# Gated cross-attention and RWKV feed-forward: the first layer norm folded into the query weights and the score bias, queries in 512-column products

## The reference

```python
xn = layernorm(x)                                   # (x - mean) / sqrt(var + 1e-5), no weights
Q, K, V = xn @ W_q.T, ctx @ W_k.T, ctx @ W_v.T      # 16 heads of 32
s = Q @ K.T / sqrt(32) - slope[head] * (qpos - kpos)        # masked keys: -inf
e = exp(s - max(s)); attn = e / (1 + sum(e))
x = x + tanh(g_xattn) * ((attn @ V) @ W_o.T)
y = layernorm(x); y_prev = y shifted by one token
xr, xk = mu_r * y + (1 - mu_r) * y_prev, mu_k * y + (1 - mu_k) * y_prev
x = x + tanh(g_ffn) * sigmoid(xr @ W_r.T) * (relu(xk @ W_k2.T) ** 2 @ W_v2.T)
```

## Time and profile before

| | |
|---|---|
| median of 3 runs | 1484.07 us (1483.07 to 1484.63) |
| profiled execution | 1483.82 us, of which its span 1482.0 us |
| busy: TensorE, weight loads | 1381.9 us (93%), 1087.4 us (73%) |
| busy: VectorE, ScalarE, GpSimd | 1009.0 us (68%), 887.6 us (60%), 717.5 us (48%) |
| mean granted clock of TensorE | 0.991 of full speed |
| x tiles loaded | 64 of 256 KB, 3.0 us from issue to landing |

### The profile page before, as it was taken

One profiled execution on the slowest core, in us unless ns is written; L12 is line 12 of the kernel. 1 busy time (PEld: TensorE's weight loads), 2 busy tenths in 40 slices (PEclk: granted clock), 3 DMA queues, 4 the chain that ended last, 5 costly groups with the idle time before them and its releaser, 6 DMA issues.

```text
span 1482.0 us, 33624 instructions
## 1 busy us (share of the span) xinstructions
PE 1381.9 (93%) x10864; PEld 1087.4 (73%) x10864; DVE 1009.0 (68%) x3658; ACT 887.6 (60%) x2931; POOL 717.5 (48%) x766
## 2 busy tenths in 40 slices
PE   7999899899999989999998989999999999999988
PEld 6876768677776867767686767767686777778667
DVE  5435858586685858677585868769585866858565
ACT  5247375665747466574747567474756657474652
POOL 0103555645545554655545464545556455455542
PEclk9999999999999999999999999999999999999999
DMA  8721001020100102010010202010020202001000
GB/s 267 222 76 43 15 21 60 0 64 14 57 21 28 50 0 78 0 57 21 28 50 14 64 0 57 21 46 32 16 62 0 64 14 57 21 28 50 4 27 29
DMA packets 53010, 65.96 MB, mean 45 GB/s; under 512 B 23024, under 2 KB 29168, under 8 KB 52976
## 3 DMA queue, kind: packets, MB, share of 16 engines
q1 hardware_dynamic: 52976, 65.52, 15.2%
HBM read 40.87 MB, written 24.64 MB: 44 GB/s over the span
## 4 chain that ended last, share of the span: by engine, by line
PE 43%; DVE 17%; issue 15%; POOL 9%; ACT 9%; DMA 5%; SPq 0%; DVEq 0%; POOLq 0%; ACTq 0%
PE rotating L401 27%; PE probs_bank L561 8%; ACT probs L775 5%; PE attn_bank L575 4%; POOL square L1368 4%; DVE diff L1109 3%; POOL xnt_or_act L1370 3%; DVE relu L1109 3%; DMA xs<-in_x_dram 2%; DVE square L1104 2%; PE score_bank L401 2%; DVE norm L1026 2%; POOL probs L1331 1%; DVE mix_k L1104 1%; POOL mixed_key L1358 1%
## 5 line engine op out<-in xcount | busy, mean ns | idle before, releaser
L775 ACT ACTIVATE probs<-probs,neg_max 128x120 f32<-128x120 f32 x1024 | 391.0, 386 | 19.6 <-DVE neg_max L1048 19.6
L1331 POOL TENSOR_TENSOR probs<-probs,recip 128x960 f32<-128x960 f32 x128 | 229.4, 1792 | 259.9 <-DVE recip L1062 259.9
L401 PE MATMUL rotating<-mixed_key,w_key 128*128 128x512 f32 x720 | 197.7, 414 | 36.5 <-ACT gated L827 36.5
L401 PE MATMUL rotating<-w_proj,attn_t 128*128 128x512 f32 x768 | 209.8, 413 | 20.6 <-ACT gated L827 18.6
L783 ACT COPY probs_t<-probs_bank 120x512 f32<-120x512 f32 x256 | 149.9, 585 | 116.8 <-PE probs_bank L561 116.4
L1048 DVE CUSTOM_DVE_ANT_0 probs<-score_bank,mask_in 128x120 f32<-128x120 f32 x1024 | 215.0, 275 | 4.3
L401 PE MATMUL rotating<-w_value,xnt_or_act 128*128 128x512 f32 x720 | 203.4, 411 | 5.5 <-POOL xnt_or_act L1370 5.3
L401 PE MATMUL rotating<-xnt_or_act,w_query 128*128 128x256 f32 x1536 | 198.7, 286 | 0.5 <-DVE xnt_or_act L1032 0.5
L775 ACT ACTIVATION_READ_ACCUMULATOR probs<-probs,neg_max 128x1 f32 x1024 | 194.7, 190 | 0.0
L401 PE MATMUL rotating<-w_gate,mixed_gate 128*128 128x512 f32 x768 | 189.7, 399 | 0.0
L401 PEld LDWEIGHTS rotating<-xnt_or_act,w_query 128*128 128x128 f32 x1536 | 187.8, 191 | 1.9 <-DVE xnt_or_act L1032 0.8
(11 more groups left out here) (126 smaller groups left out, 2162.6 us busy)
## 6 DMA issues: line engine op xcount, KB each, us to landing
xs<-in_x_dram SPq DMA_DIRECT2D x64, 256.0 KB, 3.0
out_dram<-gated SPq DMA_DIRECT2D x64, 256.0 KB, 3.0
value_scratch<-gated SPq DMA_DIRECT2D x16, 240.0 KB, 2.9
mask_in<-in_mask_dram SPq DMA_DIRECT2D x16, 240.0 KB, 2.7
keys_t<-key_scratch SPq DMA_DIRECT2D x16, 240.0 KB, 3.4
values<-value_scratch SPq DMA_DIRECT2D x16, 240.0 KB, 3.7
probs<-in_ctx_t_dram SPq DMA_DIRECT2D x6, 480.0 KB, 7.2
key_scratch<-query_t SPq DMA_DIRECT2D x12, 240.0 KB, 5.0
```

The source lines that it names most:

```text
L401: mm = pe.matmul(bank, stationary(a, c), moving(b, c), start=(i == 0), stop=(i == MATMULS - 1))
L775: e = act.activation(probs[:, t % 2, head, :], probs[:, t % 2, head, :], ACT.Exp, bias=neg_max[:, t % 2, head:head + 1], scale=-1.0, accum ...
L1331: pool.tensor_tensor(part, part, recip[:, t % 2, heads].unsqueeze(2).to_broadcast((P, H // 2, NK)), ALU.mult)\
```

## The change

x comes from the host a second time, transposed (`x_t`, one contiguous 128x512 block per tile), and SP loads it (`load_xt`) into two buffers `x_turned`. ScalarE casts a tile's high part straight from there (`xt_split`), GpSimd makes the low part (`xt_rest`); `normalise1`, `turn1`, `turn1_out` and `turn1_low` are gone. The mean is taken out of W_q instead: in start-up TensorE forms the column mean of W_q (four float32 matmuls with a constant 1/512), VectorE subtracts it before W_q is split. The factor rstd moves behind the scores: GpSimd's `rstd1_of` makes rstd and its inverse and `score_scale` = -slope * rstd for 16 heads; `bias` takes that as its scale operand, and `distances` multiplies the distances by the inverse. `query(b, m)` makes one 128-channel result for all 512 tokens, 12 matmuls of 512 columns, once all four low parts are there, and `scores` of tile 0 need all four. `turn2(0)` moves from before `proj(1)` to after `gate(3)` and all `turn2` use spare banks, so the rotation of the others shifts. On GpSimd `edge(0)` and `difference(0)` move behind `rstd1_of(1)` and `xt_rest(2)`. The diff, cut to this:

```diff
@@ uses of the rotating banks, spare banks
-    ("proj", 0, 0), ("value", 0, -1), ("value", 1, -1), ("gate", 2, -1), ("turn2", 0, 0), ("proj", 1, 0),
-    ("value", 2, -1), ("gate", 3, -1), ("proj", 2, 0), ("turn1", 1, 1),
+    ("proj", 0, 0), ("value", 0, -1), ("value", 1, -1), ("gate", 2, -1), ("proj", 1, 0),
+    ("value", 2, -1), ("gate", 3, -1), ("proj", 2, 0),
...
@@ SP
+            def load_xt(b, t):
+                sp.dma_start(x_turned[:, t % 2], x_t[bass.ds(b, 1), t].rearrange("b p c q -> (b p) c q"))\
+                    .then_inc(xt_loaded[t % 2], 16)
...
             load_mask(0)
+            for t in range(2):
+                load_xt(0, t)
...
+            for t in range(2, QT):
+                sp.wait_ge(xt_low, t - 1)
+                load_xt(0, t)
...
+            def turned_ahead(b):
+                for t in range(2):
+                    sp.wait_ge(xt_low, b * QT + t + 3)
+                    load_xt(b + 1, t)
...
                     if t == 1 and not last:
+                        for n in range(2, QT):
+                            sp.wait_ge(xt_low, (b + 1) * QT + n - 1)
+                            load_xt(b + 1, n)
@@ TensorE
             chunk(0, 0, True)
+            pe.wait_ge(averaging_ready, 1)
+            pe.wait_ge(raw_weight[0], 32)
+            for c in range(CT):
+                mm = pe.matmul(probs_bank[:], averaging, xs[:, 0, c, :], start=(c == 0), stop=(c == CT - 1))
+            mm.then_inc(wq_mean_done, 1)
             chunk(0, 1, False)
...
-                if t % 2 == 0 and g % 2 == 0:
-
-                    pe.wait_ge(read["query"], b * 4 + t + g // 2 + 1)
+                if t == 0:
+                    pe.wait_ge(read["query"], b * 4 + g + 1)
...
+            def query(b, m, steps):
+
+                if steps[0] == 0:
+                    pe.wait_ge(xt_low, (b + 1) * QT)
+                return product(bank_of["query", m][:], lambda s, c: w_query[:, s, c, m * P:(m + 1) * P],
+                               lambda s, c: xt_or_act[:, s, c, :], steps)
...
                 use("gate", 2)
-                use("turn2", 0)
                 use("proj", 1)
                 with_attention(2, "value", 2)
                 use("gate", 3)
-                use("turn1", 0)
+                use("turn2", 0)
                 use("turn2", 1)
                 with_attention(3, "proj", 2)
-                use("turn1", 1)
                 use("value", 3)
                 use("proj", 3)
-                use("turn1", 2)
+                use("turn2", 2)
                 use("query", 0)
...
-                use("turn2", 2)
-                use("query", 1, range(7))
-                use("turn1", 3)
-                use("query", 1, range(7, MATMULS))
+                use("query", 1)
                 use("turn2", 3)
@@ ScalarE
                 act.wait_ge(raw_weight[i % 2], 16 * (i // 2 + 1))
+                if raw[i] is wq:
+                    act.wait_ge(wq_centred, 1)
...
+            def xt_split(b, t):
+                act.wait_ge(xt_loaded[t % 2], b * 32 + (t // 2 + 1) * 16)
...
+                act.copy(xt_or_act[:, HI, :, t * P:(t + 1) * P], x_turned[:, t % 2]).then_inc(xt_high, 1)
...
                 feed_forward((gate_out, 2))
-                turn2_out(b, 0)
+                if ffn:
+                    after((xt_split, 0), (xt_split, 1))
...
                 feed_forward((gate_out, 3))
+                if not ffn:
+                    after((xt_split, 0), (xt_split, 1))
+                after((xt_split, 2))
+                turn2_out(b, 0)
                 probs_out(b, 3, 0)
-                after((turn1_out, 0))
+                turn2_out(b, 1)
                 probs_out(b, 3, 1)
-                turn2_out(b, 1)
...
+                after((xt_split, 3))
                 turn2_out(b, 2)
-                after((turn1_out, 3), (query_out, 1))
+                after((query_out, 0))
...
+                after((query_out, 1))
                 turn2_out(b, 3)
-                after((query_out, 2))
                 mix_key_high(b, 2)
                 mix_gate_high(b, 2)
-                after((query_out, 3))
+                after((query_out, 2), (query_out, 3))
@@ VectorE
+                    dve.wait_ge(scale1_ready, b * QT + t + 1)
...
-                                                 in1=neg_dist[:, t, :], scale=-SLOPES[head], scalar=BIG,
+                                                 in1=neg_dist[:, t, :], scale=score_scale[:, t, head:head + 1], scalar=BIG,
...
+                dve.wait_ge(dist_plain, b + 1)
+                dve.wait_ge(rstd1_ready, (b + 1) * QT)
+                dve.tensor_tensor(neg_dist, neg_dist, rstd1[:, :, 1:2].to_broadcast((P, QT, NK)), ALU.mult)\
+                    .then_inc(dist_ready, 1)
...
+            dve.wait_ge(wq_mean_done, 1)
+            dve.tensor_tensor(xs[:, 0], xs[:, 0], probs_bank[:].unsqueeze(1).to_broadcast((P, CT, D)), ALU.subtract)\
+                .then_inc(wq_centred, 1)
             weight(2)
@@ GpSimd
+                pool.wait_ge(rstd1_ready, b * QT + t + 1)
+                if earlier(b, 0, 1):
+                    pool.wait_ge(scores_biased, ((b - 1) * QT + t + 1) * G)
+                apart(pool)
+                pool.tensor_scalar(score_scale[:, t, :], neg_slopes[:], rstd1[:, t, 0:1], None, ALU.mult)\
+                    .then_inc(scale1_ready, 1)
+
+            def xt_rest(b, t):
+                pool.wait_ge(xt_high, b * QT + t + 1)
+                part = xt_or_act[:, :, :, t * P:(t + 1) * P]
+                pool.tensor_tensor(part[:, LO], x_turned[:, t % 2], as_f32(part[:, HI]), ALU.subtract).then_inc(xt_low, 1)
...
                 normalise_probs(b, 2, 1)
-                edge(b, 0)
-                difference(b, 0)
+                if ffn:
+                    after((xt_rest, 0), (xt_rest, 1))
                 rstd2_of(b, 1)
                 normalise_probs(b, 3, 0)
                 normalise_probs(b, 3, 1)
                 after((rstd1_of, 1))
+                if not ffn:
+                    after((xt_rest, 0), (xt_rest, 1))
+                after((xt_rest, 2))
+                edge(b, 0)
+                difference(b, 0)
+                after((rstd1_of, 2))
                 edge(b, 1)
                 difference(b, 1)
-                after((rstd1_of, 2))
+                rstd2_of(b, 2)
                 mix_low(b, 0)
-                rstd2_of(b, 2)
+                after((xt_rest, 3), (rstd1_of, 3))
```

More of the change, by code:

```diff
@@ L191, in flamingo_block @@
         late_read = sem("late_read")
-        done = {k: sem(f"{k}_done") for k in ("key", "gate", "value", "proj", "query", "turn1", "turn2")}
-        read = {k: sem(f"{k}_read") for k in ("key", "gate", "value", "proj", "query", "turn1", "turn2")}
-        turn1_high = sem("turn1_high")
+        done = {k: sem(f"{k}_done") for k in ("key", "gate", "value", "proj", "query", "turn2")}
+        read = {k: sem(f"{k}_read") for k in ("key", "gate", "value", "proj", "query", "turn2")}
         scores_done = sem("scores_done")
@@ L547, in late_product @@
                 return mm
-            made = {"key": key, "gate": gate, "value": value, "proj": proj, "turn1": turn1, "turn2": turn2,
+            made = {"key": key, "gate": gate, "value": value, "proj": proj, "turn2": turn2,
                     "query": query}
@@ L660, in _ @@
             pe.wait_ge(ident_ready, 1)
[L661 to L663 removed]
+            first = [u for u in ATTENTION_AND_FFN if u[0] == "query"]
             for u in range(4):
@@ L1205, in batch @@
                 mix(b, 0)
-                after((turn1_low, 0), (normalise1, 1), (statistics1, 2))
+                after((statistics1, 2))
                 residual(b, 2)
```

152 lines of the change are left out of this document (59 added, 93 removed).

## The result

The changed kernel takes 1562.74 us (median; 1560.91 to 1572.43) where the kernel before, beside it, takes 1484.35: a ratio of 1.054, with a 95% interval of 1.050 to 1.059. The profiled execution took 1560.91 us, with a span of 1559.1 and a granted clock of 0.975.

A forecast was written before the change was run, and what follows sets the result against it. Two paths ending within 2.5 us bound it: TensorE's stream, and finish(3), load of x(3), mixes, key(0). On 1483.8: 14 x 2.4 = 33.6, start-up 12 + 6.8, batch 0 4, last batch -0.6, together 55.8: 1540 us, range 1496 to 1572.

The forecast's parts named there:

- edge(0) and what waits for it: GpSimd, loop batch: memset done at 322.6 behind new work, so TensorE's third probability transpose at 323.8, +2.0 us.
- proj(1)'s wait: TensorE before proj(1): the 1.23 us wait goes and turn2(0) moves away; of 1.7 us some 0.6 is left.
- finish(3) and the port: VectorE's finish(3) meets GpSimd's mix_low(0): a two-input instruction stands still, priced 0 to 1.3 us, taken as 0.5.
- From there to key(0): Loop batch, from statistics1(3) on: 0.3 us more up to mix(1) and 0.6 for the added instruction in distances.
- One sign that I had named for being wrong: TensorE, loop batch: key(0) without a gap before it would show the prediction wrong.
- Batch 0: First batch: xt_rest 0 to 2 and a late load delay it some 9 us, partly hidden: +4, bounds 0 and 9.
- Start-up: Before the first scores: W_q centring and the queues behind it +12 us, first queries and slower matmuls +6.8.
- The +4.6 for the two buffers: First query waits for transposed tiles loaded only when xt_rest(0,0) and (0,1) free their buffers: 88.0 instead of 83.42.
- The last batch: End of the kernel: no x left to prepare there, so -0.6 us.
- Rival A: Loop faster: edge(0) in time, GpSimd there by 320.0, -2.8 us a batch, 1466 us; chance 0.07.
- Rival B: Loop breaks even: the attention's +2.0 is given back before key(0), only start-up and batch 0 stay, 1507 us; chance 0.17.
- Rival C: Worse: new waits bring TensorE's clock down, a product costs 1.2 to 1.5 us more per batch, 1560 us; chance 0.16.

The follow-up runs named there:

- edge(0) first: On GpSimd, edge(0) and difference(0) of the loop batches went ahead of rstd1_of(1) and xt_rest(2), against the changed kernel: 1512.33 us.
- the run with own buffers: Against the changed kernel, transposed tiles 2 and 3 of the first batch were loaded ahead of the fifth context chunk into diff and mix_k: 1564.43 us.
- the combination of all steps: Changed kernel with edge(0), query_out, mix(1), xt_rest(3), gate_out(0) earlier, batch 0 reordered, W_q mean inside first chunk, separate buffers loaded behind context: 1468.98 us.

## Why the prediction was right, and where its terms were off

The direction, the mechanism and the range held: 1562.7 against a forecast of 1540 and an upper end of 1572. The forecast is 22.7 low, and its terms show where. In the loop I give times on the clock of before (29.88 less, the distance of the two key(0)).

- *edge(0) and what waits for it.* Forecast: memset done at 322.6, third transpose at 323.8. Measured: 323.05 and 324.25. normalise_probs(3,1) ended at 320.2 (forecast 319.8), and rstd1_of(1) was 1.58 instead of 1.35 (the pow over two columns 0.72, where one column took 0.57, and 0.25 of waiting on itself); xt_rest 1.26 instead of 1.30. My estimate from the "GPSIMD Engine Reference" of the Trainium skill, section 3.1, was 1.1; the trace, with 1.26 here and 1.45 for xt_rest(3), stays with the row. Undoing this one step returned all of the loop's loss: shown.
- *proj(1)'s wait.* I let 0.6 of 1.7 survive. The second probability transpose of tile 2 came at 309.94 (forecast 309.65), after a wait of 1.50 on probs_out: the new wait took the place of the old one.
- *finish(3) and the port.* I took 0.5 of a range to 1.3. finish(3)'s second instruction took 1.68 beside mix_low(0), which had begun 0.17 earlier, where it took 0.75 before: 0.93. The page "SBUF — State Buffer" of the Trainium skill, section "SBUF: two separate sides", says that of a VectorE instruction with two SBUF inputs and a GpSimd one that reads SBUF, the one that starts second stands until the first is done. The trace agrees: on its own clock mix_low(0)'s first instruction ends at 362.58, and 0.75 from there would be 363.33, where finish(3)'s ended at 363.13. With this wait statistics1(3) is at 336.48; forecast 335.8.
- *From there to key(0).* Forecast +0.9, measured +1.15. In all +3.3 a batch, forecast +2.4, inside the bounds; 14 times 0.9 is 13 of the 22.7. One sign that I had named for being wrong came all the same: key(0) has no gap before it (387.53 above). It does not speak against the chain through the mixes. TensorE is held earlier, at the second half of scores(0), by query_out(2), which stands on ScalarE behind mix_gate_high(2), and gate_out(0) ends at 387.48, just ahead of key(0). My own sum had both paths end together, so I should not have named that sign.
- *Batch 0.* Forecast +4, measured +8.9 (+7.7 from first scores(0) to first scores(0)), near the upper bound. I let five of nine microseconds vanish because key(0) had no x(3) to wait for; the step failed because the attention itself stood behind the load in ScalarE's queue.
- *Start-up.* The four float32 matmuls took 3.60; I took 1.8, the upper end of my own bounds, so the true price lay outside them. chunk(0,1) came at 31.81 (forecast 30.0), the fifth chunk +13.7 (+12), first query 101.48 (100), first scores +19.9 (+18.8). The +4.6 for the two buffers was the right sum for a wrong split: 2.4 for the buffers, 2.0 for the four rests in line.
- *What the sum did not have.* The bias instruction's 61 ns, on 64 instructions a batch, was not costed at all. It was harmless (no gain could be told without it), but I had not checked that. The last batch was put at -0.6; with the tail it came to +1.7. And the lower end of the range was added up wrongly: its terms, the loop at -0.5 a batch and start-up at 6.5 and 3, with batch 0 and the last batch as forecast, give 1490 and not 1496.
- *Rival A* asked for edge(0) by 320 and priced that at -2.8 a batch. With edge(0) in time, the loop came out at 85.2: the price was wrong, because TensorE then waits for xt_rest(3), query_out(2) and gate_out(0). The batch came near what A had said, 82.9 against 82.5, only when the order of these was changed too, and at the full granted clock.
- *Rival B* did not come: nothing of the shift was given back before key(0).
- *Rival C* was seen and cost little there: 24 products took 7.33 instead of 5.74 once in most batches, yet from one key(0) to the next the four batches of the loop at a mean clock of 1.00 take 88.3 to 88.4, and nine at 0.98 take 88.3 to 89.6, 0.4 more in the mean (the last one, at 0.94, takes 91.9). Where another chain sets the batch, most of the slower matmuls lie in its shade. They cost some 1.5 us a batch where that chain had been shortened. That C's figure, 1560, is the nearest to the measured one is chance.

## What to carry to other kernels

When work is moved between engines, follow the one small instruction at the end of the queue that receives it: 1.58 + 1.26 us of new work ahead of a memset of 0.1 cost 3.3 us a batch, on an engine that is busy 53% of the run, and a change of order alone gave it back. A saving on the busiest engine is worth nothing as long as a second chain ends with it; find that chain first, and price the gain with the waits that come next. Work at the start-up is not paid by its duration but by the queues behind it: 5.9 us cost 11.3.

## What the runs showed of the hardware

The bias instruction takes 336 ns with its scale in SBUF and 275 with a constant, on the same 128x120 tile. A float32 matmul of 128x512 shows as two records, and four of them take 3.60 us, where twelve of the form used elsewhere take 2.85. TensorE's granted clock fell behind waits in some batches and not in others of the same kernel, at places that move with the order of the work: in the changed kernel at query(0), behind waits of 1.38 and 0.41 us, with edge(0) first at gate(0), behind one of 1.27. What decides that, no run here settles. Two loads of 256 KB of transposed x, issued beside the start-up's other traffic (in the run with own buffers), took 7.7 and 7.9 us to land by the list of DMA issues, where the median of the others is 3.0; issued behind the context, in the combination of all steps, they took 4.3 and 4.5.
